# Base rows kept in SBUF, h5 transposed into buffers of its own, expert weight halves split inside the channel mix, its last sums tile by tile

## What is computed

```python
h = _layernorm(x, axis=-1) * (1 + ca) + sa
x = x + ga * attn(h)                    # time mix, then channel mix:
#   kk = mix(h) @ Wkey.T ; kv = silu(kk) @ Wval.T ; x = x + sigmoid(mix(h) @ Wcr.T) * kv
h = _layernorm(x, axis=-1) * (1 + cb) + sb
sh_mid = gelu(einsum('th,ehd->ted', h, Wsh_up))
shared_out = einsum('ted,edh->th', sh_mid, Wsh_down)
probs = softmax(h @ W_router)
top_v, top_i = top_k(probs, 2)
rt_mid = gelu(einsum('th,ehd->ted', h, Wrt_up))
routed_out = einsum('ted,edh->th', rt_mid * gate, Wrt_down)
x = x + gb * (shared_out + routed_out)
```

## Time and profile before

| | us |
|---|---|
| median of 3 executions | 1032.2 (1030.53 to 1033.18) |
| profiled execution, its own time | 1036.36 |
| its span, from the first to the last instruction | 1034.6 |

### The profile page before, as it was taken

How to read it: one execution, slowest core, us unless ns; L and a number is a source line. 1 busy time by engine, 2 the same in 40 slices (tenths; PEclk the granted TensorE clock), 3 DMA queues, 4 the chain that set the end, 5 groups by cost and what they waited for, 6 DMA issues and landing times.

```text
span 1034.6 us, 13888 instructions
## 1 busy us (share of the span) xinstructions
PE 912.5 (88%) x4264; PEld 730.3 (71%) x4265; DVE 545.5 (53%) x991; ACT 381.1 (37%) x630; POOL 392.5 (38%) x309
## 2 busy tenths in 40 slices
PE   7896889999989999999999999997707999999853
PEld 2564678787768888878878887875606777787632
DVE  5896988976661115342632264154752444443638
ACT  2664473746455432222221321343112333332321
POOL 3331100000124471450153025254466888870740
PEclk9899889999989999999999999998957999999957
DMA  8558566671445361620162143326654766775752
GB/s 347 164 167 258 187 205 202 200 227 42 143 163 163 102 194 51 201 104 30 52 194 82 51 150 115 112 88 198 219 165 148 249 231 230 221 251 194 232 182 94
DMA packets 110017, 170.90 MB, mean 165 GB/s; under 512 B 8696, under 2 KB 53752, under 8 KB 109200
## 3 DMA queue, kind: packets, MB, share of 16 engines
q1 hardware_dynamic: 62352, 115.74, 33.8%
q0 software_dynamic: 10464, 35.66, 10.7%
q10 hardware_dynamic: 37152, 18.88, 6.1%
HBM read 100.72 MB, written 69.52 MB: 165 GB/s over the span
## 4 chain that ended last, share of the span: by engine, by line
PE 66%; DVE 15%; issue 6%; DMA 6%; ACT 3%; another core or an unknown queue 2%; POOL 1%; SPq 1%; DVEq 0%; ACTq 0%
PE kv_ps L412 5%; PE kk_ps L412 5%; PE kk_ps L414 5%; PE kv_ps L414 5%; PE kk_ps L413 5%; PE kv_ps L413 5%; PE mm_ps L412 4%; PE mm_ps L413 4%; PE mm_ps L414 4%; PE up_ps L412 3%; PE dn_ps L412 2%; PE up_ps L413 2%; PE up_ps L414 2%; DVE raw_ps L1337 2%; PE dn_ps L414 2%
## 5 line engine op out<-in xcount | busy, mean ns | idle before, releaser
L1537 DVE TENSOR_TENSOR silu<-kk_ps,silu 128x512 fp32r<-128x512 f32 x64 | 44.2, 691 | 220.1 <-ACT silu L2135 205.8
L2131 ACT ACTIVATE kk_ps<-kk_ps 128x512 f32<-128x512 f32 x64 | 37.2, 582 | 215.4 <-PE kk_ps L414 207.0
L412 PE MATMUL kv_ps<-cm_w,silu 128*128 128x512 f32 x256 | 100.8, 394 | 0.0
L412 PE MATMUL kk_ps<-xk,cm_w 128*128 128x512 f32 x256 | 100.5, 393 | 0.0
L414 PE MATMUL kv_ps<-cm_w,silu 128*128 128x512 f32 x256 | 99.8, 390 | 0.0
L414 PE MATMUL kk_ps<-xk,cm_w 128*128 128x512 f32 x256 | 99.7, 390 | 0.0
L413 PE MATMUL kk_ps<-xk,cm_w 128*128 128x512 f32 x256 | 99.6, 389 | 0.0
L413 PE MATMUL kv_ps<-cm_w,silu 128*128 128x512 f32 x256 | 99.6, 389 | 0.0
L1831 DVE TENSOR_TENSOR xsT<-xs_ps,xsT 128x512 fp32r<-128x512 f32 x42 | 29.0, 692 | 93.7 <-ACT xsT L2218 93.7
L2308 POOL TENSOR_TENSOR rs<-mv,neghalf 128x4 f32<-128x4 f32 x12 | 13.6, 1134 | 161.7 <-DVE mv L1266 161.6
L2301 POOL TENSOR_TENSOR cm_w<-stage,cm_w 128x1024 fp32r<-128x1024 f32 x16 | 38.6, 2423 | 91.4 <-ACT cm_w L1922 91.4
(11 more groups left out here) (259 smaller groups left out, 2380.7 us busy)
## 6 DMA issues: line engine op xcount, KB each, us to landing
xs_s<-zero ACTq DMA_DIRECT2D x13, 1024.0 KB, 6.1
stage<-in_wex POOLq DMA_DIRECT2D x26, 512.0 KB
xsb<-xs_s SPq DMA_DIRECT2D x44, 256.0 KB, 3.3
ys_s<-ysb SPq DMA_DIRECT2D x41, 256.0 KB, 2.2
stage<-in_wcm SPq DMA_DIRECT2D x16, 512.0 KB, 4.0
wmod<-in_wmod SPq DMA_DIRECT2D x6, 1024.0 KB, 11.8
stage<-in_wtm SPq DMA_DIRECT2D x10, 512.0 KB, 4.6
ys_s<-zero ACTq DMA_DIRECT2D x5, 1024.0 KB, 5.4
```

The costliest lines, as they stand in the source:

```text
L412: pe.matmul(out, lhs[0], rhs[0], start=first, stop=False)
L1537: dve.tensor_tensor(silu[:, g % NSILU, 1, :], kk_ps[g % 2][:, :], silu[:, g % NSILU, 0, :].bitcast(F32), ALU.subtract).then_inc(s_silo, 1)
L2131: act.activation(kk_ps[g % 2][:, :], kk_ps[g % 2][:, :], ACT.Silu).then_inc(s_silu, 1)
```

## The change

- Base rows: `base8` holds the eight rows of batches 0 and 1 in SBUF; `store_base` and `base_s` are gone, `load_x4` loads all eight x4 tiles into buffers that are free by then, `combine_b` reads `base8`; `bsb` holds and loads only the rows of batches 2 and 3. SyncE no longer waits for base stores ahead of `load_xs`.
- h5T of the last two tiles is written to `h5b`; the shared expert's input of a batch is loaded at once (`load_ht`) into the low half of its own `ht`, and split there in place; `ht` of batch 1 has a buffer of its own, that of batch 3 is loaded at the start of the expert loop into part of `mid`. `ht_lo` of batch 1 moves from GpSimd to VectorE.
- Halves 26 to 30 are split by ScalarE in steps 11 to 15 of the last batch, 31 to 33 between its first operations behind it.
- The last two value groups go out together, tile by tile (`last_values`, semaphore `s_kvt`), and post work waits for its tile.
- `route` moves to step 6, `place_a` to `place_c` and `prefix_sums` to step 7.
- TensorE's, VectorE's, ScalarE's, GpSimd's and SyncE's order behind the channel mix is rewritten.
- In the tail `g2b` has all 16 tiles, `NG` is 8, and a gather waits for the scaling of the tile eight before (`s_o1`), not for its sum (`s_o4`).

```diff
+            def load_ht(b):
+                for i in range(2):
+                    sp.wait_ge(s_h5Tst[i], 32 * (b + 1))
+                if b == 0:
+                    sp.wait_ge(s_kk, (NB - 1) * MF + 12)
+                elif b == 1:
+                    sp.wait_ge(s_kvt, TT)
+                elif b == 2:
+                    sp.wait_ge(s_up, KT)
+                else:
+                    sp.wait_ge(s_dn, SB * TT)
+                for k in range(KT):
+                    sp.dma_start(ht_of(b)[:, 1, k].bitcast(F32), h5T_s[b, :, k, :]).then_inc(s_h5r[b % 2], 16)
+            def load_x4(tiles):
+                for t in tiles:
+                    sp.wait_ge(s_x4st[t % TT], 16 * (t // TT + 1))
+                    if t == 0:
+                        sp.wait_ge(s_kk, NB * MF)
+                    if t == TT:
+                        sp.wait_ge(s_xklo, NB * KT)
+                    if t == TT + 2:
+                        sp.wait_ge(s_x4, NT)
+                    sp.dma_start(x4_of(t), x4_s[t]).then_inc(s_x4l, 16)
...
+            load_ht(0)
+            for n in range(28, 34):
                 load_half(n, ex_half(n))
+            load_ht(1)
             last = NT - TT
             store_x4(last)
             store_x4(last + 1)
             store_h5T(last)
+            load_x4(range(TT))
+            store_h5T(last + 1)
             store_x4(last + 2)
+            load_ht(2)
             store_x4(last + 3)
             store_h5T(last + 2)
             store_h5T(last + 3)
+            load_x4(range(TT, SB * TT))
+            load_half(34, ex_half(34))
+            load_half(35, ex_half(35))
+            load_gb(1)
...
-            for i in range(TT):
-                sp.wait_ge(s_basest[i], 16 * SB)
             load_xs(0, 0)
             load_xs(1, 1)
             load_xs(2, 0, 1)
             load_xs(3, 1, 2)
+            load_ht(NB - 1)
...
+            def last_values():
+
+                pe.wait_ge(s_sihi, NB * MF)
+                pe.wait_ge(s_silo, NB * MF)
+                for j in range(TT):
+                    for g in (NB * MF - 2, NB * MF - 1):
+                        m = g % MF
+                        a = [silu[:, g % NSILU, i, j * P:(j + 1) * P] for i in range(2)]
+                        w = [cm_unit(2 * (m // KT) + 1)[:, i, m % KT, :] for i in range(2)]
+                        mm = mm3(pe, kv_ps[j][:, :], a, w, False, m == MF - 1)
+                        if j == TT - 1 and m < MF - 1:
+                            mm.then_inc(s_kv, 1)
+                    mm.then_inc(s_kvt, 1)
...
             first, rest, every = range(KT - 1), [KT - 1], range(KT)
-            shared_up(0, [0, 1, 2])
+            shared_up(0, [0, 1])
             turn5(last)
+            shared_up(0, [2])
+            router(last)
+            turn5(last + 1)
             shared_up(0, [3])
-            router(last)
-            shared_down(0, [0, 1], first)
-            turn5(last + 1)
-            shared_down(0, [0, 1], rest)
             router(last + 1)
-            shared_down(0, [2], every)
             turn5(last + 2)
-            shared_down(0, [3], [0, 1])
+            shared_down(0, [0], every)
             router(last + 2)
             turn5(last + 3)
-            shared_down(0, [3], [2, 3])
+            shared_down(0, [1], [0, 1])
             router(last + 3)
-            shared_up(1, [0])
+            shared_down(0, [1], [2, 3])
+            shared_down(0, [2], every)
+            shared_down(0, [3], every)
             prefix_sums(NB - 1)
-            shared_up(1, [1, 2, 3])
+            shared_up(1)
...
+                if b and m == 6:
+                    route(b - 1)
                 if b and m == 7:
-                    route(b - 1)
-                if b and m == 8:
                     place_a(b - 1)
...
+            mid_lo(0)
             post_a(t + 2)
             post_b(t + 2)
+            post_d(t + 1)
             post_c(t + 2)
-            post_d(t + 1)
+            mid_lo(1)
             post_a(t + 3)
             post_b(t + 3)
+            post_d(t + 2)
+            post_c(t + 3)
+            mid_lo(2)
+            post_d(t + 3)
             mid_lo(3)
-            post_c(t + 3)
-            post_d(t + 2)
-            post_d(t + 3)
+            ht_lo(1, range(KT))
             route(NB - 1)
             place_a(NB - 1)
+            place_b(NB - 1)
             mid_lo(4)
...
+            gb_shared(3)
+            table_a()
+            mid_lo(7)
+            table_b()
+            ht_lo(2, range(KT))
+            table_c()
+            gb_shared(4)
+            gates_a()
+            gb_shared(5)
+            table_d()
+            base_add(0)
+            gb_shared(6)
             base_add(1)
...
+                if b == NB - 1 and m == 11:
                     weight_hi(26)
                     weight_hi(27)
+                if b == NB - 1 and m == 12:
+                    ht_hi(0, [0, 1])
+                if b == NB - 1 and m == 13:
+                    ht_hi(0, [2, 3])
+                    weight_hi(28)
+                if b == NB - 1 and m == 14:
+                    weight_hi(29)
+                if b == NB - 1 and m == 15:
+                    weight_hi(30)
...
+            weight_hi(31)
             gelu(0, [0])
+            weight_hi(32)
+            gelu(0, [1])
+            weight_hi(33)
             to_h5T(last)
+            ht_hi(1)
+            gelu(0, [2])
+            to_h5T(last + 1)
             gelu(0, [3])
...
-            ht_lo(0, [0, 1])
             weight_lo(26)
             weight_lo(27)
-            ht_lo(0, [2, 3])
+            ht_lo(0)
+            weight_lo(28)
+            weight_lo(29)
+            weight_lo(30)
             post_rsqrt(NT - 4)
             weight_lo(31)
+            for t in range(NT - 3, NT):
+                post_rsqrt(t)
             weight_lo(32)
+            weight_lo(33)
             scatters(NB - 1)
+            weight_lo(34)
+            weight_lo(35)
...
                 if t >= NG:
-                    pool.wait_ge(s_o4, t - NG + 1)
-                for c, buf in ((0, g1b[:, t]), (1, g2b[:, t % NG])):
+                    pool.wait_ge(s_o1, t - NG + 1)
+                for c, buf in ((0, g1b[:, t]), (1, g2b[:, t])):
```

More of the change, by code:

```diff
@@ L42 @@
 ERING = RING - BASE
-NG = 9
+NG = 8
 NSILU = 4
@@ L324, in adaln_block @@
         s_gb = sem("s_gb")
-        s_x4l = [sem("s_x4l0"), sem("s_x4l1")]
-        s_basest = [sem(f"s_basest{i}") for i in range(TT)]
+        s_x4l = sem("s_x4l")
         s_sub = sem("s_sub")
@@ L445, in h5_row, with h5T_of, x4_of @@
             return stage[:, j // 2, (j % 2) * H:(j % 2 + 1) * H]
+        def h5T_of(t):
+            if t >= NT - 2:
+                return h5b[:, t % 2].rearrange("p (k c) -> p k c", c=P)
+            return h5T[:, t % 2]
+        def x4_of(t):
+            return x4h[:, t] if t < TT else x4m[:, t - TT] if t < TT + 2 else x4n[:, t - TT - 2]
         def gathered(t):
             i = t % NG
-            before = 32 * NB if i < TT else 0 if i < TT + 2 else 16 * (NE - PRE) if i < TT + 4 else 16 * (NT + NB)
+            before = 32 * NB if i < TT else 0 if i < TT + 2 else 16 * (NE - PRE)
             return before + 32 * (t // NG + 1)
@@ L456, in mid_of, with ht_of @@
         def mid_of(b):
-            return mid[:, (b if b < SB else b - SB) % 2]
+            return ht if b == NB - 1 else mid[:, b % 2]
+        def ht_of(b):
+            return {1: ht1, NB - 1: mid[:, 1]}.get(b, ht)
         def dn_of(t):
@@ L1041, in router @@
                 for k in range(KT):
-                    mm = pe.matmul(rt_ps[:, t, :], h5T[:, t % 2, k, :], wrt[:, k, :], start=k == 0, stop=k == KT - 1)
+                    mm = pe.matmul(rt_ps[:, t, :], h5T_of(t)[:, k, :], wrt[:, k, :], start=k == 0, stop=k == KT - 1)
                 mm.then_inc(s_rt, 1)
@@ L1053, in prefix_sums @@
                     .then_inc(s_pf, 1)
-            for g in range(NB * MF + 2):
+            for g in range(NB * MF):
                 b, m = divmod(g, MF)
@@ L1060, in _ @@
                     value(g - 2)
-                if g < NB * MF:
-                    key(g)
-                if b and g < NB * MF:
+                key(g)
+                if b:
                     if m == 4:
@@ L1695, in ht_lo @@
             def ht_lo(b, tiles):
+                if b == 1 and 0 in tiles:
+                    dve.wait_ge(s_htlo, KT)
+                hi, lo = (ht_of(b)[:, i] for i in range(2))
                 for k in tiles:
-                    n = b * KT + k
-                    dve.wait_ge(s_hthi, n + 1)
-                    dve.tensor_tensor(ht[:, 1, k, :], h5r[:, n % 2], ht[:, 0, k, :].bitcast(F32), ALU.subtract)\
+                    dve.wait_ge(s_hthi, b * KT + k + 1)
+                    dve.tensor_tensor(lo[:, k, :], lo[:, k, :].bitcast(F32), hi[:, k, :].bitcast(F32), ALU.subtract)\
                         .then_inc(s_htlo, 1)
@@ L1864, in combine_a @@
                 dve.wait_ge(s_o1, t + 1)
```

(7 more changed lines are left out.)

238 lines of the change are left out of this document (77 added, 161 removed).

## The result

The changed kernel takes 1009.24 us (median of 4, 1006.41 to 1010.1) against 1032.29 (1030.53 to 1033.18) for the kernel before beside it: ratio 0.9774, 95% interval 0.975 to 0.9798. It is 23 us faster, where 38 were forecast, and lies 2 us outside the range. The profiled execution took 1009.81 us, its span is 1008.1.

A forecast was written before the change was run, and what follows sets the result against it. TensorE was taken as busy in channel mix and loop, loose in the transition and tail. Gains of 34.5 + 4 = 38.5 us took the profiled 1036.4 to 997.9, or 994 after the 4.2 offset from the median; range 975 to 1007.

The forecast's parts named there:

- U: Milestone: start of the loop's first up matmul; the forecast had TensorE's loop start 34.5 us earlier.
- E: Milestone: end of the last subtraction on turned rows; the forecast had the tail gain 4 us.
- The choice a step earlier: Channel mix: routing at step 6 meets GpSimd, TensorE waits 2.1 to 2.4 us in three batches; costs 2.5 us.
- Weight halves at no cost: Channel mix, steps 11 to 15: ScalarE splits halves 26 to 30, costed at nothing, at most 5 us.
- last values tile by tile: End of channel mix: tile 0 done at 678.4, VectorE starts 4.1 us earlier, TensorE's end unchanged.
- The walk through the transition: Channel mix to loop: TensorE starts the loop at 743.8 instead of 778.35, gain 34.5 us, bounds 27 and 40.
- rival D: Transition: first expert rows still held by SyncE, start moves only about 18 us: 1014 us; chance 0.04.
- B: Transition: in-order waits, such as two ht loads landing 5 us late each, cost 10 us: 1006 us; chance 0.18.
- rival C: Transition: code loads stall if DMA share reaches about 0.9, two stalls of 20 us: 1034 us; chance 0.03.
- The eight adds (0.69 each) no longer wait for a load or a store: Transition, VectorE's base-row adds: 0.69 us each, three ahead of the last gb product, done at 739.3.
- The tail: After the loop: ScalarE's 19.67 us gap moves as its code is needed later, TensorE's crawl stays; gain 4 us, bounds 0 and 21.
- Rival A: Tail: ScalarE's gap and TensorE's crawl both vanish, gain 21 us instead of 4: 977 us; chance 0.14.

The follow-up runs named there:

- r2: The changed kernel run again unaltered, on a chip where the kernel before took 1013.8 us: 992.12 us.
- r5: The changed kernel run again unaltered, beside a kernel before at 1032.3 us: 1008.28 us.
- e9: Changed kernel with GpSimd's weight splits 34 and 35 waiting for VectorE's low halves of ht for batch 2: 979.19 us, kernel before 1013.8.
- e10: Changed kernel with e9's wait, choice and positions at steps 7 and 8, gates' last steps behind the first turned-row subtraction, gathers unpaced: 990.17 us, before 1032.3.
- e1: Changed kernel with VectorE's last four base adds and gates moved behind the first turned-row subtraction: 1003.71 us, kernel before 1033.7.
- e2: Changed kernel with GpSimd's first expert split waiting for all eight base adds instead of four: 997.05 us, kernel before 1033.7.
- e6: Changed kernel with e2, e4, e9's wait, choice at step 7, positions at step 8, gates behind the first turned-row subtraction: 975.88 us, before 1014.1.
- e11: e10 with the gathers of tile t waiting for those of tile t-2: 973.91 us, kernel before 1032.3.
- e4: Changed kernel with gathers of tile t waiting for those of t-2, at most four under way: 992.32 us, kernel before 1033.7.
- r4: Kernel before with the gathers of tile t waiting for those of tile t-2: 1016.04 us, plain kernel before 1032.3.

## Why the forecast was right or wrong

**The sum, closed.** On the profiled executions 38.5 us were forecast and 26.5 measured (1034.6 less 1008.1). By milestones: U came 22.4 us earlier where 34.5 were forecast for the start (12.1 missing); U to E took 169.2 instead of 168.4 (0.8 missing); E to the end 80.2 instead of 85.1, 4.9 against 4 (0.9 too much). The last 3.6 us of the miss are no mechanism: the profiled execution of before lay 4.2 over its median, that of the changed kernel 0.6.

**The choice a step earlier: right.** Forecast 2.1 to 2.4 us a wait; measured 6.6 us for three, 2.2 each. The route of batch 0, which runs during batch 1, from VectorE's time line:

```profile
438.58 0.96 DVE L1610 TENSOR_TENSOR oh<-rev,top 128x64 f32<-128x64 f32 x1
...
440.95 1.21 DVE L1608 TENSOR_TENSOR lg<-lg,rev 128x64 f32<-128x64 f32 x1
...
443.44 1.31 DVE L1621 TENSOR_TENSOR chosen<-oh 128x64 bf16<-128x64 f32 x1
```

Operations of 0.22 held up to 1.31, as rows 7 had it. The same three waits of the channel mix came to 4.1 and 2.5 us in two traces of the kernel before and to 6.6, 5.9 and 5.7 in three of the changed one (as first shown, r2, r5), so the cost of the step is 1.6 to 4.1 us against a forecast of 2.5.

**Weight halves at no cost, last values tile by tile: right.** VectorE's post work begins at 680.55; 678.4 plus the 2.5 above is 680.9. The last value matmul starts at 684.20, 2.1 us later than before, no more than the choice a step earlier accounts for.

**The walk through the transition: right to 3 us.** With 2.5 added to each forecast: scatters 729.2, measured 729.97; positions 718.8, measured 720.57; table 737.9, measured 740.60; last gb product 741.8, measured 743.77; TensorE's turn of the first rows 743.8, measured 744.54. The meeting with passes 34 and 35 was foreseen, on the wrong victim: not `ht_lo(2)` for 3.6 us but L1775 for 4.8. That the turn is right to 0.7 is in part luck: the rows were asked for 3.2 us later than forecast (741.94, not 738.7), and they landed in 2.6 us or less where 5 were put down. Passes that stayed in VectorE's post chain still met it: L1557 took 2.72 us at 684.42 and L1581 1.96 at 699.43. Rows were asked for 1.3 us behind the table, so rival D is out; ScalarE's longest wait for an ht was 2.77 us, so B's late transfers are out; the DMA share was 0.61 instead of the 0.79 of rival C. The 0.9 by which C was to be decided is misread besides: the 0.94 of the earlier trace rows is that of 970 to 975, and in ScalarE's gap itself, from 977.25, the share was 0.77.

**The signs.** TensorE's wait for the rows (5.5) and its waits for the choice (2.2 each) are as foretold. The wait for h5T was to vanish and fell from 5.4 to 1.8. The table was to be written 21 us earlier and is 16 (740.60 against 756.80), for the 2.5 us of the choice and the late steps above.

**The step that failed: "The eight adds (0.69 each) no longer wait for a load or a store".** It was priced by an add alone, and the walk ended at the last gb product, for which TensorE waits. Two things were left out. The adds of tiles 4 to 7 and the gates stand behind that product but ahead of `turned_lo(0)` on the same engine. And the fourth add is what lets GpSimd's splits go, so that the adds behind it meet them: 10.4 us instead of 2.4. The forecast had weighed this very contention twice, in the route and in passes 34 and 35, and counted GpSimd's earlier start only as something that might be late itself. TensorE's turn to its first `up` takes 14.2 us, 2.8 before. That is the 12.1 missing: 0.7 up to the turn, 11.4 behind it. In e9, with the same order and no split beside the last adds and the gates, it takes 4.5: so 9.7 of the 11.4 are the length of these operations beside GpSimd, and 1.7 their place in the queue. The forecast amounts to 746.6 for U (743.8 and the 2.8 of before) and holds 3.6 for a meeting that e9 has not, so to 743 on e9's terms. e9's trace shows 742.20, but with positions 4.1 us earlier than those of the changed kernel for no reason of the edit; without that it would be 746.3, and the agreement is luck. The price could have been read from the trace of the kernel before, where an add of base rows, beside two weight passes, took 2.65 us:

```profile
753.97 5.10 POOL L2301 TENSOR_TENSOR ex_w<-stage,ex_w 128x1024 fp32r<-128x1024 f32 x2 [11.55 <-ACT ex_w L1922]
...
756.97 2.65 DVE L1718 TENSOR_TENSOR yb<-yb,x4l 128x512 f32<-128x512 f32 x1
```

The list of signs that would show the forecast wrong named waits on ht, mid and s_exr; a wait on `xsT` wasn't in it.

The Trainium skill (SBUF — State Buffer, SBUF: two separate sides) says that whichever of the two engines starts first has the port pair for its whole instruction. An add that takes 2.4 to 2.8 beside splits of 1.9 and 2.7 agrees. L1775 at 5.00 us beside two passes of 4.74 together does not: it waited for two instructions, not one, and by the records it had started first (730.73 against 730.96). The measurement decides.

**GpSimd's first split: 22.0 us earlier (744.07), 24.5 forecast.** It waited for the fourth add, not for its weights. Nothing in the loop waited for a weight.

**The tail: the size right, the reason wrong.** Forecast: ScalarE's gap leaves its place because its next code is needed later. Measured: 18.29 us, at the same operation as before, the first gelu of the last batch.

```profile
972.13 0.58 ACT L2200 ACTIVATE up_ps<-up_ps 128x512 f32<-128x512 f32 x1 [18.29 <-remote]
```

TensorE, meanwhile, with nothing named that it waits for:

```profile
967.67 0.59 PE L419 MATMUL up_ps<-mid,ex_w 128*128 128x512 f32 x1 [0.81 <-issue]
969.07 0.59 PE L420 MATMUL up_ps<-mid,ex_w 128*128 128x512 f32 x1 [0.81 <-issue]
970.47 0.59 PE L421 MATMUL up_ps<-mid,ex_w 128*128 128x512 f32 x1 [0.81 <-issue]
```

The place in the program did not decide; the gathers did. Not all of the gap is unnamed: the gelu needs twelve matmuls of TensorE, which crawled out between 953.62 and 963.4, so 8.8 us of the 18.29 are left with no reason in the trace. In e10 it is 11.1, in the kernel before 19.1, and in e1 nothing, where the view names TensorE's product for all of 20.19. What these traces share is the end. In the seven with the stall no gather packet moves any more when it ends: ScalarE goes on 0.6 to 1.2 us after the last one in six of them (971.1 and 972.13 here, 950.9 and 951.54 in e10), and in e1 TensorE is back at its pace about a microsecond after 964.3. So the forecast's "behind gather packets" agrees with the traces, but its carrier does not. Code loads are not supported: e10's trace has no packet on an instruction queue from 937 to 951, while ScalarE waits until 951.54. The Trainium skill (Runtime: NRT & Kernel Launch, Instruction fetch mechanics), as cited in the prediction, calls code blocks mostly hidden; by that rule the gap would not be a code load, and no run speaks against that. What it waits for was not found, nor why the stall is missing on two of the four chips. The 4.9 us gained have no share in this: without the stall it is 2.9, where the tail is shorter because half of the base rows are no longer loaded or ht is there sooner; which of these was not tried. Rival A's mechanism (a free tail) was real, 17 us, but nothing in the change brings it about; it took a wait of its own.

## What to carry to other kernels

When a wait goes, walk each engine's queue on to the next thing that the bottleneck needs, not only to the end of the step that was shortened, and ask of every two-input SBUF operation on the way whether GpSimd will now be running beside it; holding GpSimd back by one small wait (e2, e9) won 12 to 13 us, more than reordering VectorE (e1, 5.5). Queue gathers a few at a time: it cost 2 to 3 us where nothing stalled and saved 16 where it did. And run the kernel before beside every set: it differed here by 18 us between sets, each on another chip, more than most of the edits are worth. A single profiled execution needs the same care: e9's ran 6.3 us ahead of r2's before its edit could act.

## What was not expected of the hardware

- A two-input SBUF operation of one element a row on VectorE took 5.00 us beside GpSimd's two back-to-back passes (4.74), 4.97 to 5.00 in ten traces, and 0.16 with GpSimd quiet, in four (e6, e9, e10, e11). A 128x512 add took 0.67 and 2.4 to 2.8; operations with an input in PSUM kept 0.67 to 0.69 in both.
- With 26 gathers or more issued in a row, ScalarE stood 18 to 20 us, up to 19 of them for nothing that the trace names, and TensorE's matmuls came mostly 0.4 to 1.4 us apart, until the last gather packet had passed, in some sets of runs; in others the same programs had neither (tail 63.6 instead of 80.2 us). At most four under way avoided it each time it was tried where the kernel before had it (e4, e11, r4).
